# Attention values as three rounded-float products instead of one float32 product, in a kernel of top-k mask, modulated norm and attention

## The reference

```
adj  = s * cond * softmax(x) / sqrt(N), diagonal = -inf      # s [N,1], cond [1,N]
x    = x + mask of the 10240 largest entries of adj
xn   = rms_norm(x) * g * (1 + scale) + shift                 # scale, shift = cond @ W_emb + b
q,k,v = xn @ W_qkv, 16 heads of 64; q, k = rms_norm * gains
o    = softmax(q k^T / 8) v
out  = x + o + o @ W_out
```

## Time and profile before

| | |
|---|---|
| median of 3 runs | 4088.08 us (4087.03 to 4089.53) |
| profiled execution | 4087.43 us |
| its span | 4085.7 us |
| granted TensorE clock, mean over the span | 0.959 |
| instructions | 44416 |

### The profile page before, as it was taken

How to read it: one execution, slowest core, us unless ns; L and a number is a source line. 1 busy time by engine, 2 the same in 40 slices (tenths; PEclk the granted TensorE clock), 3 DMA queues, 4 the chain that set the end, 5 groups by cost and what they waited for, 6 DMA issues and landing times.

```text
span 4085.7 us, 44416 instructions
## 1 busy us (share of the span) xinstructions
PE 3797.2 (93%) x16035; PEld 2457.0 (60%) x16035; DVE 2589.9 (63%) x4521; ACT 1545.2 (38%) x2727; POOL 1283.3 (31%) x1907
## 2 busy tenths in 40 slices
PE   5885899999988899999989899999989899999999
PEld 2334666666644667766644677777644677666744
DVE  8996777777774777777774677777775322322221
ACT  1005444444423444444422444444432344444430
POOL 1005433333303533333312533333312433333310
PEclk9996899999998899999999799999999799999999
DMA  4002010000134000010024100000124100000023
GB/s 156 0 15 103 16 37 21 21 21 21 34 133 147 16 21 21 27 31 21 21 101 154 55 21 21 21 21 21 37 71 161 31 21 21 21 21 21 21 81 99
DMA packets 179360, 195.25 MB, mean 48 GB/s; under 512 B 7576, under 2 KB 137680, under 8 KB 178128
## 3 DMA queue, kind: packets, MB, share of 16 engines
q1 hardware_dynamic: 179152, 192.55, 14.9%
HBM read 144.29 MB, written 48.23 MB: 47 GB/s over the span
## 4 chain that ended last, share of the span: by engine, by line
PE 73%; DVE 14%; ACT 5%; POOL 4%; issue 3%; DMA 1%; SPq 0%; DVEq 0%; POOLq 0%; ACTq 0%
PE pax L1003 24%; PE ppv L1072 18%; PE pst L1058 10%; PE pst L991 10%; PE pax L1038 7%; DVE mx L823 3%; DVE xr L718 3%; DVE trash L683 3%; PE pax L1021 2%; POOL xn L379 1%; PE pax L1046 1%; PE pax L1096 1%; ACT sA L545 1%; ACT pt L552 1%; DVE otok L838 1%
## 5 line engine op out<-in xcount | busy, mean ns | idle before, releaser
L1003 PE MATMUL pax<-wh,xn 128*128 128x384 f32 x3840 | 1058.1, 347 | 11.8 <-issue 8.8
L1072 PE MATMUL ppv<-pt,v 128*65 128x512 f32 x2048 | 987.8, 594 | 1.0 <-DVE otok L838 1.0
L683 DVE TENSOR_SCALAR_CACHE_REDUCE trash<-keys,state 128x2048 uint8<-128x2048 f32 x384 | 899.8, 2343 | 9.9
L823 DVE TENSOR_REDUCE mx<-pax 128x1 f32<-128x512 f32 x960 | 617.9, 685 | 222.6 <-PE pax L1038 202.2
L1003 PEld LDWEIGHTS pax<-wh,xn 128*128 128x128 f32 x3840 | 704.7, 189 | 22.9 <-issue 19.6
L552 ACT ACTIVATE pt<-pst 128x1024 f32<-128x1024 f32 x512 | 524.5, 1024 | 503.9 <-PE pst L1058 445.7
L1003 PE MATMUL pax<-wl,xn 128*128 128x384 f32 x1920 | 649.3, 338 | 0.0
L809 DVE TENSOR_REDUCE ss<-sq 128x4 f32<-128x256 f32 x256 | 107.2, 419 | 782.2 <-ACT sq L527 782.2
L1038 PE MATMUL pax<-sA 65*128 65x512 f32 x960 | 473.3, 540 | 28.3 <-ACT sA L540 17.5
L1072 PEld LDWEIGHTS ppv<-pt,v 128*65 128x65 f32 x2048 | 278.5, 137 | 297.2 <-issue 221.7
L351 POOL TENSOR_TENSOR wl<-wf,wh 128x1024 fp32r<-128x1024 f32 x99 | 235.9, 2387 | 586.1 <-ACT wh L468 586.1
(11 more groups left out here) (139 smaller groups left out, 4445.0 us busy)
## 6 DMA issues: line engine op xcount, KB each, us to landing
wf<-in_L_cond_W_qkv SPq DMA_DIRECT2D x99, 512.0 KB, 5.4
keys<-in_x SPq DMA_DIRECT2D x32, 512.0 KB, 8.9
xin<-in_x SPq DMA_DIRECT2D x32, 512.0 KB, 4.0
out_x<-xin SPq DMA_DIRECT2D x32, 512.0 KB, 2.6
wo<-in_L_cond_W_out SPq DMA_DIRECT2D x4, 4096.0 KB, 13.6
pt<-out_x SPq DMA_DIRECT2D x64, 256.0 KB, 3.9
out_x<-pt SPq DMA_DIRECT2D x64, 256.0 KB, 2.5
oT_scr<-ostg SPq DMA_DIRECT2D x56, 256.0 KB, 2.0
```

What stands on the lines that cost most here:

```text
L683: e.tensor_scalar(trash[:], kv, thr_f, None, ALU.is_ge, ALU.add, accum_out=cnt[:, c:c + 1]).then_inc(z_cnt, 1)
L823: e.tensor_reduce(mx2[:, j // T, j % T, c:c + 1], max_banks(alone, j)[:, c, :], axis=AX, op=ALU.max).then_inc(m_mx, 1)
L1003: i = e.matmul(qkv_bank(alone, t)[:, 0:6 * DH], xn[:, a, k, t * P:(t + 1) * P], w[:, k, :, :].rearrange("p s c -> p (s c)"), start=(k == 0 ...
L1072: i = e.matmul(ppv[0:DH + 1, c, :], v2[:, par, kt, hh, :], pt[:, kt % 2, c * HALF:(c + 1) * HALF], start=(kt == 0), stop=(kt == T - 1))
```

## The change

It does five things.

1. **Values.** v is kept as a rounded-float high part `vh` (with the ones) and a low part `vl`; the probabilities as `ph`, a float32 copy `pf` (ScalarE takes the exp twice) and `pl`, GpSimd's difference (`low`). A value step is `vh`x`ph`, `vl`x`ph`, `vh`x`pl`, two matmuls each. The first four wait for the first exp (`t_eh`), the last two for the low part (`t_lo`); what `fill` puts between stands ahead of the last two.
2. **v in the preparation.** ScalarE copies q, k and v in one operation; GpSimd rounds and splits v, two more operations per tile.
3. **Order.** In the second half score step t+2 follows value step t; the places of the maxima are new. GpSimd's row memsets stand after tile 1 of the pair.
4. **Weights.** All 8 pairs' weights are split once, during `search_alone`, and stored in memory; a pair then loads 3 MB of finished parts.
5. **Low features.** `xn`'s low half is stored in memory by 16 DMAs per sequence and comes back 0.5 MB per tile into a ring of three (`xl`), 4 MB per pair. The projection's order is now product by product, and only its last 8 matmuls wait for `xl`. In `prep_alone` the loads of the first three tiles stand ahead of the keys.

```diff
-    xn = inner.enter_context(nc.sbuf_tensor("xn", [P, 2, KT, N], F32R))
+    xh = inner.enter_context(nc.sbuf_tensor("xh", [P, KT, N], F32R))
+    xl = inner.enter_context(nc.sbuf_tensor("xl", [P, 3, KT, P], F32R))
+    vh = inner.enter_context(nc.sbuf_tensor("vh", [P, 2, T, 2, DH + 1], F32R))
+    vl = inner.enter_context(nc.sbuf_tensor("vl", [P, 2, T, 2, DH], F32R))
+    ph = inner.enter_context(nc.sbuf_tensor("ph", [P, 2, N], F32R))
...
+    pl = inner.enter_context(nc.sbuf_tensor("pl", [P, 2, N], F32R))
...
+            for m, i in enumerate(SPLIT_ORDER):
+                wait(e, d_wst, 32 * m)
+                for c in range(3):
+                    e.dma_start(wf[:, :, c, :], wqkv_v[:, :, c, i, :]).then_inc(d_w, 16)
+                e.wait_ge(w_l, 3 * (m + 1))
+                e.dma_start(w_scr[i, :, 0, :], w_high.bitcast(F32)).then_inc(d_wst, 16)
+                e.dma_start(w_scr[i, :, 1, :], w_low.bitcast(F32)).then_inc(d_wst, 16)
...
         def load_w(self, i):
-            for s in range(3):
-                self.e.dma_start(wf[:, :, s, :], wqkv_v[:, :, s, i, :]).then_inc(d_w, 16)
+            self.e.dma_start(w_high.bitcast(F32), w_scr[i, :, 0, :]).then_inc(d_w2, 16)
+            self.e.dma_start(w_low.bitcast(F32), w_scr[i, :, 1, :]).then_inc(d_w2, 16)
+
+        def load_xl(self, gp, t):
+
+            e, u = self.e, T * gp + t
+            wait(e, a_qkv, u - 2)
+            e.dma_start(xl[:, u % 3].rearrange("p k c -> p (k c)").bitcast(F32), xl_scr[t]).then_inc(d_xl[u % 3], 16)
...
+                if fb is not None and t % 4 == 3:
+                    self.store_xl(fb, t // 4)
...
+            e, gp = self.e, PAIRS * b
+            for t in range(T):
+                if t % 4 == 0:
+                    for r in range(4):
+                        e.wait_ge(d_xst[r], 32 * (2 * b + t // 4 + 1))
+                self.load_xl(gp, t)
+                if t == 2 and kb is not None:
+                    e.wait_ge(f_xr, T * (b + 1))
+                    self.load_keys(kb)
+            e.wait_ge(a_qkv, T * (gp + 1))
             self.load_w(1)
...
+            if prep:
+                for t in range(3):
+                    self.load_xl(gp + 1, t)
...
+                for t in range(3, T):
+                    self.load_xl(gp + 1, t)
+                e.wait_ge(a_qkv, T * (gp + 2))
...
+            for m in range(PAIRS):
+                self.split_w(m)
...
+            e.tensor_copy(vh[:, par, t, :, 0:DH], v).then_inc(a_vh, 1)
+            e.wait_ge(a_vh, u + 1)
+            e.tensor_tensor(vl[:, par, t], v, vh[:, par, t, :, 0:DH].bitcast(F32), ALU.subtract).then_inc(a_vs, 1)
+
+        def low(self, gp, hh, kt):
+
+            e, w = self.e, T * (2 * gp + hh) + kt
+            e.wait_ge(t_ex, CST + w + 1)
+            e.tensor_tensor(pl[:, kt % 2, :], pf[:, kt % 2, :], ph[:, kt % 2, :].bitcast(F32),
+                            ALU.subtract).then_inc(t_lo, 1)
...
-            self.split_w(gp + 1)
 
         def pair(self, b, i, par, search, prep, first):
             e, gp = self.e, PAIRS * b + i
-            if prep:
-                self.prep_rows(gp + 1, 1 - par, T * (gp + 1))
-            else:
-                wait_apart(e, d_wo, 16 * (b + 1), passed)
+            self.low(gp, 0, 0)
+            for t in range(T):
+                self.low(gp, (t + 1) // T, (t + 1) % T)
+                if prep:
+                    self.prep_tile(gp + 1, 1 - par, t)
+                    if t == 1:
+                        self.prep_rows(gp + 1, 1 - par, T * (gp + 1) + 2)
+            if not prep:
...
-            for t in range(T):
-                if prep:
-                    self.prep_tile(gp + 1, t)
-            if prep:
-                self.split_w(gp + 2)
+            for t in range(1, T):
+                self.low(gp, 1, t)
...
-                        if not isinstance(m, int) or m > 1:
-                            wait_apart(e, f_lo, m - 1, passed)
-                        e.activation(xtmp[:, k % 2, :], ppv[:, k % 2, :], ACT.Identity,
+                        wait(e, d_xst[k % 4], 16 * (m // 4))
+                        e.activation(xtmp[:, k % 4, :], ppv[:, k % 2, :], ACT.Identity,
...
-            e.activation(pt[:, kt % 2, :], pst[:, 2 * (kt % 2):2 * (kt % 2) + 2, :].rearrange("p a b -> p (a b)"),
-                         ACT.Exp, scale=DH ** -0.5).then_inc(t_ex, 1)
+            src = pst[:, 2 * (kt % 2):2 * (kt % 2) + 2, :].rearrange("p a b -> p (a b)")
+            e.activation(ph[:, kt % 2, :], src, ACT.Exp, scale=DH ** -0.5).then_inc(t_eh, 1)
+            e.activation(pf[:, kt % 2, :], src, ACT.Exp, scale=DH ** -0.5).then_inc(t_ex, 1)
...
+            if t == 0 and gp == 0:
+                e.wait_ge(w_l, 3 * PAIRS)
+            elif t == 0:
+                e.wait_ge(d_w2, 32 * gp)
             elif t > 1 or not alone:
-                e.wait_ge(a_v, u - 1 if alone else u)
-            for k in range(KT):
-                for m, (a, w) in enumerate(((0, wh), (0, wl), (1, wh))):
-                    i = e.matmul(qkv_bank(alone, t)[:, 0:6 * DH], xn[:, a, k, t * P:(t + 1) * P],
+                e.wait_ge(a_qk, u - 1 if alone else u)
+            for m, (a, w) in enumerate(((xh[:, :, t * P:(t + 1) * P], wh), (xh[:, :, t * P:(t + 1) * P], wl),
+                                        (xl[:, u % 3], wh))):
+                if m == 2:
+                    e.wait_ge(d_xl[u % 3], 16 * (u // 3 + 1))
+                for k in range(KT):
+                    i = e.matmul(qkv_bank(alone, t)[:, 0:6 * DH], a[:, k, :],
                                  w[:, k, :, :].rearrange("p s c -> p (s c)"), start=(k == 0 and m == 0),
...
-            e.wait_ge(t_ex, CST + w + 1)
+            if kt == 0:
+                e.wait_ge(a_vs, T * (gp + 1))
+            e.wait_ge(t_eh, w + 1)
             for c in range(2):
-                i = e.matmul(ppv[0:DH + 1, c, :], v2[:, par, kt, hh, :], pt[:, kt % 2, c * HALF:(c + 1) * HALF],
-                             start=(kt == 0), stop=(kt == T - 1))
-                if c == 0 and between is not None:
-                    between()
+                e.matmul(ppv[0:DH + 1, c, :], vh[:, par, kt, hh, :], ph[:, kt % 2, c * HALF:(c + 1) * HALF],
+                         start=(kt == 0), stop=False, skip_group_check=True)
+            for c in range(2):
+                e.matmul(ppv[0:DH, c, :], vl[:, par, kt, hh, :], ph[:, kt % 2, c * HALF:(c + 1) * HALF],
+                         start=False, stop=False, skip_group_check=True)
+            if between is not None:
+                between()
+            e.wait_ge(t_lo, CST + w + 1)
+            for c in range(2):
+                i = e.matmul(ppv[0:DH + 1, c, :], vh[:, par, kt, hh, :], pl[:, kt % 2, c * HALF:(c + 1) * HALF],
+                             start=False, stop=(kt == T - 1), skip_group_check=True)
             i.then_inc(t_pv, 1)
...
-            e.wait_ge(f_lo, 2 * KT * (b + 1))
+            e.wait_ge(f_ev, 2 * KT * (b + 1))
...
+            gaps = [None, *range(T), None, "row", *range(T, 2 * T), None] if prep else [None] * (3 * T - 4)
...
-            self.scores(gp, par, 1, 2)
-            self.values(gp, par, 1, 0)
-            if search and not prep:
-                self.search_sum(STEPS * b + 4 * i + 1)
-            if prep:
-                self.transpose_tile(gp + 1, T - 1)
-            self.values(gp, par, 1, 1)
-            fill()
-            for t in range(2, T):
-                if t < T - 1:
-                    self.scores(gp, par, 1, t + 1)
+            for t in range(T):
+                self.values(gp, par, 1, t, fill if t > 0 else None)
+                if t == 0 and prep:
+                    self.transpose_tile(gp + 1, T - 1)
+                if t + 2 < T:
+                    self.scores(gp, par, 1, t + 2)
+                if t > 0:
                     fill()
-                self.values(gp, par, 1, t, fill)
-                fill()
-                if search and not prep and t in (4, 7):
-                    self.search_sum(STEPS * b + 4 * i + {4: 2, 7: 3}[t])
+                if t > 1:
+                    fill()
+                if search and not prep and t in (0, 4, 7):
+                    self.search_sum(STEPS * b + 4 * i + {0: 1, 4: 2, 7: 3}[t])
 
...
```

93 lines of the change are left out of this document (49 added, 44 removed).

## The result

The changed kernel takes **4357.78 us** (median of 4 runs, 4346.01 to 4361.87) against 4087.56 (4 runs beside it): a ratio of 1.0655, 95% interval 1.0634 to 1.0677. The forecast was 4325, in a range from 4185 to 4440. The profiled execution took 4361.9 us, its span is 4360.0, 274.3 more than before.

The account below looks back on a forecast made before the run. TensorE was taken as the bound, at 93% of the span. Preparing pairs +144 (28 x 5.1), non-preparing pairs +27, first search +42 and boundaries +27 make 240 on 4087.4, rounded to 4325 us, range 4185 to 4440.

Parts of the forecast that it names:

- (a): Tiles 1 to 7 of a preparing pair's first half: low part covered, value steps 0.33 us shorter, gain 2.3 us per pair.
- (b): First value step of a pair: it waits for the second exp and the subtraction, loss 1.7 us.
- (c): Row memsets after tile 1 delay value step 3's low part: TensorE stands 2.8 us; tile 2's queued preparation catches up by tile 3.
- (d): Turn to the second half: two exps stand ahead of tile 7's stacking, so the maxima start 2.0 us later.
- (e): Second-half maxima: two pairs now stand together and wait for their banks, loss 0.9 us per preparing pair.
- The clock: Rival: TensorE's clock falls after the 2.8 us stand, next tile some 3 us longer, 84 us in all, 4410; chance 0.06.
- (f): Four pairs that prepare nothing: steps of 3.1 us instead of 2.65, partly hidden by VectorE's search, +27 us in all.
- (g): First search: all 24 weight splits on GpSimd add their time to VectorE's mask operations, +42 us.
- the sign that I named: First search: VectorE's mask operations would be about 42 us longer in sum if the forecast was right.
- (h): Boundaries: GpSimd's slower lone preparation, 5.9 us, and keys about 2 us late, three times 7.9 plus 3, +27 us.
- the ring of GpSimd and VectorE: Lone preparation where keys are loaded: GpSimd sets the pace, 4.76 us a tile plus 0.84.
- GpSimd as the bound of the first half: Rival: GpSimd's tile takes 7.5 us rather than 6.6 beside VectorE, 120 us more, 4445; chance 0.14.

Follow-up runs that it names:

- experiment 2: Changed kernel with GpSimd's two row memsets moved to the end of the second half in 24 of 28 preparations: 4280.4 us.
- experiment 1: Changed kernel with the last two value matmuls of first-half steps 0 to 6 in preparing pairs issued after the projection tile: 4296.4 us.
- experiment 5: Changed kernel with 21 of the 24 GpSimd weight subtractions in the first search left out, loads, roundings and stores kept: 4304.3 us.
- experiment 6: Changed kernel with the weights of pairs 1 to 7 split in the first sequence's pairs instead of the first search: 4301.1 us.
- experiment 7: Changed kernel with the first three low-feature loads and the next keys' loads issued earlier at the boundaries: 4347.0 us.
- experiment 11: Changed kernel with deferred low product, moved memsets, earlier stacking, separated maxima, weights split in pairs, earlier loads, earlier exp high, v rounded by ScalarE: 4175.7 us.
- experiment 12: Experiment 11's kernel, with GpSimd's first second-half subtraction waiting for VectorE's split of tile 7 and the last row memsets moved: 4073.3 us.
- experiment 9: Changed kernel with exp high waiting only for the last read of its slot, not the whole value step two earlier: 4357.9 us.

## Why the prediction held, and where it didn't

The direction and the cause of nearly each term stand; 240 were forecast, 270 measured. Two products of the sum are slightly off: 28 x 5.1 is 143, not 144, and 7 x 6.3 is 44, not 42. Per preparing pair the measured parts are -2.2 + 1.3 + 2.4 + 2.05 + 1.0 and 1.2 for the clock, 5.7 us where 5.1 were forecast.

- (a) -2.3: measured -2.2 (experiment 2).
- (b) +1.7: 1.3 in the mean, a wait of 1.58 in 24 of the 28; experiment 1 took it away.
- (c) +2.8: the wait is 2.14, its worth 2.36 (experiment 2). What was "queued behind" it does not catch up by itself (experiment 1).
- (d) +2.0: 2.05. (e) +0.9: 1.0 at full clock, 1.3 in the mean.
- **The clock** was put at nothing in the sum and at 0.06 as a rival. It is a part of the case: 1.45 us behind the stand of step 3 in 17 of the 28 pairs, 0.3 in the mean of the second halves, some 1.2 us per pair, which the smaller (b) and (c) hide by 0.8. That is luck. The granted clock below 1 inside pairs was on my own list of what would show me wrong. What failed is the step that took "stalls of up to 1.3 us left it at 1" and 4.09 us at 0.50 as a choice between all and nothing for 2.8; at 2.1 it is now one, now the other.
- (f) +27: the exps of the 4 pairs that prepare nothing take 50.6 instead of 45.6 us, first to last, in the first of them and 51.1 instead of 42.7 in the last; with 52.2 and 50.4 in the two between, 5.0 + 6.6 + 4.8 + 8.4 = 25.
- (g) +42: 51. That the subtractions cost it was right (experiments 5, 6), but the size came near by luck: I had put all of it on the masks, and they have 20 of it, so the sign that I named, masks 42 us longer in sum, did not come. The other 31 are short VectorE operations that a subtraction blocks and TensorE's slower clock behind the waits, which no term had.
- (h) +27: the four lone preparations take 11.8, 11.9, 11.7 and 3.3 us more, where 7.9 were forecast for each of the first three. The fourth tile's low features did not land when they were wanted, TensorE waits 3.4 to 4.5 us for them, but the ring of GpSimd and VectorE sets the end, and that wait costs nothing (experiment 7, without it, takes the same 50.8 us). The step that failed is that ring, taken as 5.60 us a tile: it added GpSimd's 0.84 to 4.76 and left out that the longer tile brings two operations together that were apart; 6.05.
- **GpSimd as the bound of the first half** (0.14) did not come: 53.60 us for eight tiles is below the 55.82 before. Its reason, though, that operations stretch each other, is a part of (g), (h) and experiment 11. The Trainium skill (SBUF — State Buffer, "Who interferes with whom") says that whoever issues first has the shared pair for the whole instruction and that the other blocks in full; the traces agree down to a product of one element per partition (1.94 us) and a split of 0.28 that took 2.42.

## What to carry to other kernels

A value that needs one more engine (here exp, exp, subtraction: 4.4 us) needs a place for each consumer, not only enough room on average: look for what stands in that engine's queue ahead of it, and move what isn't urgent (memsets, splits) to where the engine idles. Where GpSimd runs long operations on SBUF, look at each short VectorE operation on the critical path that reads two SBUF operands (here copies and a TENSOR_SCALAR of two elements were held up as well), and let GpSimd wait for it: in experiment 12 that wait gave back 100 us. Where a ring of several engines sets the pace, look for each wait on it before releasing a slot earlier (experiment 9). And price a stall of some 2 us on TensorE with the slower matmuls behind it.

## What was not expected of the hardware

- VectorE operations on one or two elements per partition (0.15 to 0.17 us) lasted 1.94 to 2.27 us beside a GpSimd subtraction of 2.39, and three in a row did so beside three subtractions.
- A shift of 0.3 us on GpSimd, less work and not more, cost 3.6 us in the mean of 28 pairs (experiments 11, 12), of which some 1.95 are the blocked split and the rest the clock behind it.
- The same stand of TensorE (2.14, 2.15 us) was followed by matmuls at full clock in one pair and by 1.5 us of delay in another. Why is open; no run tells them apart.
- With two of six value matmuls left out, the granted clock fell from 0.943 to 0.887 over the span, and half of the expected gain did not come; what the clock's share in that is, no run tells.
